# Where the expert's number is loaded in the routed jobs of an attention and mixture-of-experts kernel

## The reference, cut to what matters

```python
B, S, D, I, E, K = (4, 256, 512, 256, 8, 2)
shared = silu(x @ shared_gate_w) * (x @ shared_up_w) @ shared_down_w
logits = x @ router_w
top_val, top_idx = jax.lax.top_k(logits, K)
probs = zeros_like(logits).at[arange(T)[:, None], top_idx].set(sigmoid(top_val))
xin = probs.T[:, :, None] * x[None]
gu = einsum('etd,edf->etf', xin, gate_up_w)
gate, up = split(gu, 2, axis=-1)
h = silu(gate) * up
expert_out = einsum('eti,eid->etd', h, down_w)
combined = shared + expert_out.sum(axis=0)
```

## Time and profile before

| | us |
|---|---|
| median of 3 runs | 380.87 (380.09 to 383.15) |
| profiled execution, device time | 381.52 |
| span of its instructions in the trace | 379.8 |
| TensorE busy | 331.9 (87% of the span) |
| GpSimd busy | 209.3 (55%) |
| VectorE busy | 209.4 (55%) |
| ScalarE busy | 178.4 (47%) |

### The profile page before, as it was taken

How to read it: one execution, slowest core, us unless ns; L and a number is a source line. 1 busy time by engine, 2 the same in 40 slices (tenths; PEclk the granted TensorE clock), 3 DMA queues, 4 the chain that set the end, 5 groups by cost and what they waited for, 6 DMA issues and landing times.

```text
span 379.8 us, 6456 instructions
## 1 busy us (share of the span) xinstructions
PE 331.9 (87%) x1601; PEld 218.8 (58%) x1627; DVE 209.4 (55%) x476; ACT 178.4 (47%) x401; POOL 209.3 (55%) x196
## 2 busy tenths in 40 slices
PE   2868999999999883258999999999999999999981
PEld 1335675667667552235666666666666666666650
DVE  1755888889988469951444334444343344444331
ACT  2467687577675433512443433344434433344430
POOL 0679999877756124075254465555555455555433
PEclk9978899999999898558999999999999999999997
DMA  7856687665563405150344566656655475665635
GB/s 191 301 177 221 183 270 235 211 212 205 176 214 110 168 4 172 25 169 6 78 76 94 83 118 115 135 98 113 103 106 103 99 117 108 113 112 90 108 40 73
DMA packets 29763, 50.61 MB, mean 133 GB/s; under 512 B 5472, under 2 KB 9312, under 8 KB 29728
## 3 DMA queue, kind: packets, MB, share of 16 engines
q0 software_dynamic: 9008, 21.66, 31.6%
q1 hardware_dynamic: 19232, 27.99, 23.1%
q10 hardware_dynamic: 1488, 0.54, 0.7%
HBM read 30.45 MB, written 19.73 MB: 132 GB/s over the span
## 4 chain that ended last, share of the span: by engine, by line
PE 46%; POOL 15%; issue 13%; DMA 8%; DVE 8%; ACT 7%; ACTq 1%; POOLq 0%; DVEq 0%
PE bank L909 11%; PE bank L917 8%; PE bank L914 8%; POOL gu_lo L348 5%; DMA out_rows<-y,jscatter 5%; PE bank L936 4%; PE bank L942 4%; PE bank L939 4%; PE bank L1021 4%; POOL rstd L325 3%; POOL dn_lo L348 3%; PE bank L926 2%; POOL pen L343 2%; ACT bank L472 2%; DMA kpad_in<-in_mask_BxS_bf 2%
## 5 line engine op out<-in xcount | busy, mean ns | idle before, releaser
L425 POOL DMA_INDIRECT out_rows<-y,jscatter x39 | 61.9, 1587 | 87.5 <-DMA out_rows<-y,jscatter 60.1
L826 DVE SCALAR_TENSOR_TENSOR h<-bank,xg,h 128x256 f32<-128x256 f32 x39 | 18.9, 484 | 106.1 <-ACT h L575 93.4
L917 PE MATMUL bank<-gu_hi,x_lo 128*128 (+1 forms) x220 | 71.5, 447 | 0.0
L909 PE MATMUL bank<-gu_hi,x_hi 128*128 (+1 forms) x220 | 67.4, 429 | 3.4 <-issue 3.1
L406 POOL DMA_INDIRECT xg<-xn_rows,jgather x39 | 41.5, 1063 | 29.0 <-DVE jgather L796 14.3
L914 PE MATMUL bank<-gu_lo,x_bf 128*128 (+1 forms) x200 | 55.7, 393 | 1.3 <-issue 0.2
L348 POOL TENSOR_TENSOR gu_lo<-stage,gu_hi 128x1024 bf16<-128x1024 f32 x18 | 42.6, 2372 | 23.6 <-ACT gu_hi L477 23.5
L575 ACT ACTIVATE h<-bank,xg 128x256 f32<-128x256 f32 x39 | 18.5, 474 | 74.5 <-PE bank L917 66.3
L909 PEld LDWEIGHTS bank<-gu_hi,x_hi 128*128 128x128 f32 x220 | 39.1, 193 | 24.9 <-issue 19.5
L917 PEld LDWEIGHTS bank<-gu_hi,x_lo 128*128 128x128 f32 x220 | 42.6, 194 | 13.4 <-issue 0.8
L942 PE MATMUL bank<-dn_hi,h_lo 128*128 (+1 forms) x110 | 46.0, 499 | 0.0
(11 more groups left out here) (125 smaller groups left out, 489.8 us busy)
## 6 DMA issues: line engine op xcount, KB each, us to landing
stage<-in_L_ffn_gate_up_w SPq DMA_DIRECT2D x16, 512.0 KB, 3.7
xin<-in_x SPq DMA_DIRECT2D x16, 256.0 KB, 4.5
xn_rows<-xn SPq DMA_DIRECT2D x16, 256.0 KB, 4.1
stage<-in_L_ffn_down_w SPq DMA_DIRECT2D x8, 512.0 KB, 3.9
out_rows<-x SPq DMA_DIRECT2D x16, 256.0 KB, 4.3
out_rows<-zeros POOLq DMA_DIRECT2D x1, 1024.0 KB, 5.0
ctx_in<-in_ctx SPq DMA_DIRECT2D x1, 768.0 KB, 8.7
xg<-xn_rows,jgather POOLq DMA_INDIRECT x39
```

Of the source, the lines that this page charges most:

```text
L425: g.indirect_dma_start(out=out, out_offset=bass.IndirectOffsetOnAxis(ap=jscatter[:, n - TILES:n - TILES + 1], axis=0), in_=y[:, r, :], in_ ...
L909: tn.matmul(ps_g(n)[:], x_hi[:, n % TS, k, :], gu_hi[:, e, k, :], start=(k == 0), stop=False)
L917: last = tn.matmul(ps_g(n)[:], x_lo[:, n % TS, k, :], gu_hi[:, e, k, :], start=False, stop=(k == KC - 1))
```

## The change

In `silu` on ScalarE and in `gated` on VectorE the call of `value_load` moves from behind the waits for the producer to in front of them. Nothing is added or removed.

```diff
             def silu(n):
+                e = act.value_load(jexpert[0:1, n - TILES:n - TILES + 1], min_val=1, max_val=E)
                 act.wait_ge(g_ps, n + 1)
                 act.wait_ge(hT_ps, n - 1)
-                e = act.value_load(jexpert[0:1, n - TILES:n - TILES + 1], min_val=1, max_val=E)
                 a.activation(h[:, n % 2, :], ps_g(n)[:, 0:I], ACT.Silu,
                              scale=xg[:, n % XS, bass.ds(e + (D - 1), 1)]).then_inc(act_s, 1)
@@
             def gated(n):
+                e = dve.value_load(jexpert[0:1, n - TILES:n - TILES + 1], min_val=1, max_val=E)
                 dve.wait_ge(act_s, n + 1)
-                e = dve.value_load(jexpert[0:1, n - TILES:n - TILES + 1], min_val=1, max_val=E)
                 v.scalar_tensor_tensor(h[:, n % 2, :], ps_g(n)[:, I:2 * I], xg[:, n % XS, bass.ds(e + (D - 1), 1)],
                                        h[:, n % 2, :], ALU.mult, ALU.mult).then_inc(h_s, 1)
```

## The result

The changed kernel took 367.36 us in the median of 5 runs (365.61 to 367.94), the kernel before 381.42 us in the 5 runs beside it (380.09 to 383.15). The change was measured three more times against the kernel before, 0.966 (0.963 to 0.969), 0.971 (0.968 to 0.974) and 0.963 (0.959 to 0.968), which is 11 to 14 us.

A forecast was written before the change was run, and what follows sets the result against it. It took TensorE as the bound, stalled 0.27 us per job by the chain through ScalarE's load. Terms 1.5 + 7.0 + 0.3 + 1.15 = 10.0 us off the profiled 381.52, with its median 0.65 lower, gave 371.0 us; range 368.8 to 375.0.

The forecast's parts named there:

- What bounds the kernel: Steady stretch: TensorE looks full but stands still 0.27 us per job, waiting for the chain L917, `silu`, `x_hi`, `gate_up_high`.
- the value taken between 0.43 and 0.58: Cost of ScalarE's load behind its wait, before `silu`: taken as 0.53 us.
- TensorE late next: Steady jobs: with the stall gone TensorE's own stream sets the period, 4.75 us instead of 5.02; half of 0.53 paid out.
- The rival in which the idle time is TensorE's own: Weight loads before `gate_up_high`: their 0.43 us idle is TensorE's, so the period stays 5.02; 378 us, 6 in 100.
- The start: Job 0, where nothing hides the chain: TensorE restarts `gate_up_high` of job 1 earlier by 0.8 us.
- The first scatter: After job 0's copy of `y`: it leaves 1.5 us earlier, at 182.9 instead of 184.43.
- Jobs 0 to 10: Serial scatters and late gathers limit the gain up to job 11 to 1.5 us; TensorE waits about 2.1 and 1 us.
- Jobs 11 to 38: 27 steps, the first given nothing, the other 26 gaining 0.27 each: 7.0 us, plus 0.3 for one long load.
- a long load: Jobs 11 to 38: one load of up to 0.877 us leaves the path, counted at half its excess, 0.3 us.
- The end: After the last L917 both loads are on the path: 0.53 + 0.62 = 1.15 us gained.
- The fallen clock: Before job 10: the 2.1 us wait lowers TensorE's clock to 0.85 over 8 us; 371 to 372.5 us, 5 in 100.
- Slower scatters: First six serial steps: faster jobs load the DMA queue and lengthen landings; 377.4 us if all take 7.00, 2 in 100.

The follow-up runs named there:

- e3: The kernel before with only ScalarE's load moved in front of the waits: 369.49 us.
- e4: The kernel before with only VectorE's load moved in front of the wait: 380.2 us, ratio 0.998.
- e5: The kernel before with ScalarE's load written twice behind the wait: 407.7 us, ratio 1.073.
- e1: The kernel before, run again with a trace and no edit: 380.7 us.
- e2: The changed kernel, run again with a trace and no further edit: 367.64 us, ratio 0.966 to the kernel before.
- e11: The kernel before with 14 tiny matmuls in TensorE's idle time ahead of the last shared job's transposes: 383.29 us, ratio 1.008.
- e7: The kernel before with the first seven scatters waiting by the table of experts, four tiny DMAs at kernel start raising its counts: 383.34 us.
- e10: The kernel before with the first seven scatters waiting by the table of experts, its four tiny DMAs issued in GpSimd's idle time before the first gather: 383.16 us.
- e14: The kernel before, first seven scatters waiting by the table of experts, four one-row DMAs between job 4's gather and job 0's scatter: 379.44 us, ratio 0.998.
- e9: The changed kernel with the first seven scatters waiting by the table of experts, its four tiny DMAs in GpSimd's idle time before the first gather: 370.25 us.

## Why the prediction was wrong

**What bounds the kernel: right.** The 0.27 us stall of TensorE in front of `gate_up_high`, hidden under a busy share of 99%, was the price of the load. It is gone, and the step is 4.75 us, to the hundredth what the earlier trace rows gave. e3 and e4 show that the loop goes through ScalarE, e5 that one load on it costs 0.53, the value taken between 0.43 and 0.58.

**TensorE late next: right.** Of 0.53 us only 0.27 is paid out. The rival in which the idle time is TensorE's own (378 us) fell with e3, where the idle time went with ScalarE's load alone, and with e5.

**The start: right as far as the chain goes.** TensorE stood still for 1.67 us in front of `gate_up_high` of job 1; in the changed kernel it is 0.87, 0.80 less, the forecast:

```profile
171.38 1.20 PE L909 MATMUL bank<-gu_hi,x_hi 128*128 x4 [0.87 <-issue]
```

Where the clock was the same (before, e1, e2) the way from the first gather to `silu` 0 is 12.8 and 12.1, 0.7 shorter. The first scatter, counted from `silu` 0, is another 0.74 earlier (8.87 to 8.12); forecast 1.5 - 0.8 = 0.7.

**Jobs 0 to 10: the term that was mis-sized.** The prediction says: "The whole GpSimd chain moves only with its first scatter, by 1.5." The chain moved, as said, with its first scatter, and TensorE waits for the gathers of jobs 10 and 11. The weight loads of the transposes in the changed kernel, as in the earlier trace rows:

```profile
213.34 0.42 PEld L1021 LDWEIGHTS bank<-ident,xg 128*128 128x128 f32 x4 [1.20 <-DMA xg<-xn_rows,jgather]
...
218.92 0.42 PEld L1021 LDWEIGHTS bank<-ident,xg 128*128 128x128 f32 x4 [1.05 <-DMA xg<-xn_rows,jgather]
```

1.20 and 1.05 us, where I had 2.1 and 1. For I had kept the six serial steps at their 35.62 us, and they took 34.1 to 34.6: 1.4 us less, nearly all of it the one step of 7.00. Counted from `silu` 0, `silu` 11 came 2.8 us earlier: 0.74 by the first scatter, 1.44 by the steps, 0.53 by its own load, and 0.1. Forecast was 1.2, the 0.7 of the chain and the 0.53 of its own load, which the sum books under the end. The prediction named this ("6 steps without the one long of 7.00 give 1.3, hence 369") but put it in the range and not in the likeliest case. It was no chance row of one trace, for the kernel before shows it again in e1; the mistake was to carry it over to the changed program, where none of four traces has it. Why they have not is open (e4, e11).

**Jobs 11 to 38: right, one term by luck.** 7.6 us, forecast 7.3. All 27 steps give their 0.27, the first one too, to which I had given nothing: 7.3. The other 0.3 is one step of 5.30 in the kernel before, from `silu` 34 to 35. I had put 0.3 down to a long load, but there was none on ScalarE in these jobs; the long one of 0.877 is that of job 10. In job 35 the load took its usual time, and the address instruction (L575) came late behind the load's last instruction (L574):

```profile
L574 ACTq TENSOR_LOAD <-jexpert x1: 273/273/273, 351.8 to 351.8; - x1
L574 ACTq SEQ_ASSERT  x1: 18/18/18, 352.3 to 352.3; - x1
L575 ACTq FUSED_REGOPS  x1: 46/46/46, 352.6 to 352.6; - x1
```

In job 34 the last two both start at 347.3. The step of 5.30 is at the same place in e1, e4, e7, e10, e11 and e14, and in no trace with ScalarE's load moved. What makes the gap was not tried.

**The end:** both loads are off the path (`gated` 0.15 behind `silu`), but from `silu` 38 to the end only 0.4 us came out of the 0.62 (1.15 less the 0.53 that `silu` itself has). The last rows of the changed kernel:

```profile
356.05 0.69 DVE L835 COPY y<-bank 128x512 f32<-128x512 f32 x1 [1.09 <-PE bank L942]
357.78 1.56 POOL L425 DMA_INDIRECT out_rows<-y,jscatter  x1 [1.23 <-issue]
```

The copy of `y` comes 3.82 us after `silu` 38 where it was 4.43, so the 0.6 is there; behind it 0.2 is lost again. The scatter starts 1.04 after `y` (0.97 before), and the end is 6.1 us behind it (5.9 before).

**The sum** then is 0.7 + 2.8 + 7.6 + 0.4 = 11.5 us with the clock alike, where the prediction has 10.0. That is the low end of the four measurements (11 to 14). Taken off the 380.87 from which the prediction starts, it gives 369.4, still inside my range.

**Ahead of job 0's `silu`: the step that took the time out of the range.** The prediction changes nothing there but the chain's 0.8. It does not name that job 0's matmuls ran at 1.2 GHz in the kernel before (the clock came back at 174.0 us), and it put a change of that, and any spread, at nothing without a reason. What the runs showed: from the first gather to `silu` 0 three of the four changed traces have 9.6 to 9.7 us where the kernel before has 12.8, 3.1 less, of which 0.7 is the chain and 2.4 goes with the clock. On top of it the first gather lies up to 2 us apart in traces of the same changed kernel. That is of the size of the 2.5 us by which the medians (14.1) exceed the 11.5, but it is not traced for the execution that is the median: the traced one is the fastest of its five runs (365.61). Why the clock came back early is open.

**The fallen clock** did not come: the waits of 1 us in front of jobs 10 and 11 left it at 1.00. **Slower scatters** with faster jobs did not come either: in the steady stretch they keep the pace of the jobs (270.37, 275.10 and 279.85 us in the changed kernel).

## What to carry to other kernels

A load of a register behind a wait is paid in full by the chain behind that wait, 0.5 to 0.6 us in each use here, and in front of it nothing while the engine would idle anyway. Whether that is worth anything is told by the distance between single starts on the full engine: 99% busy by the profile hid 0.27 us of standstill in 5.02, and that, not the 0.53 us of the load, was the gain. Where a chain of DMAs sets the pace of a part and one of its steps is a quarter longer than the rest, do not carry that step over to a changed program: here it came in two traces out of two of one program and in none of the edited ones, so both values belong in the forecast. And look at the clock ahead of the part that is changed: a stretch at half the clock is 2.4 us that can come or go.

## What I had not expected of the hardware

- The same one-number load takes 0.28 to 0.30 us in most jobs and 0.8 to 1.0 in a few, on ScalarE (0.95 in e4), VectorE (0.99 in the changed kernel) and TensorE (0.95 in the kernel before). In e5 VectorE's median rose to 0.40. What lengthens it was not tried.
- With four DMAs of 128 numbers of 4 bytes ahead of it, a store of 64 KB (in rows of 32 bytes) landed after 15.4 us (e9) and 18.1 (e10) instead of 5.0.
- A step in a chain of scatters went from 7.0 and 7.2 to 5.6 us when 14 tiny matmuls were put into TensorE's idle time some 45 us earlier (e11), and to 5.7 when only VectorE's load was moved (e4). The cause is open.
